# Inverse roots as exp(-0.5 ln x) on ScalarE, the squares one step sooner, and no filler products on TensorE

## The reference

```
def _l2norm(t):
    n = jnp.sqrt(jnp.sum(t * t, axis=-1, keepdims=True))
    return t / jnp.maximum(n, EPS)
q = _l2norm(proj(Wq, bq));  k = _l2norm(proj(Wk, bk));  v = proj(Wv, bv)     # 16 heads of 8
attn = einsum('bhid,bhjd->bhij', q, k) / n ** sigmoid(m)                      # no softmax
x = x + (attn @ v) @ Wo + bo
x = x + cross_attention(ctx, ctx, layernorm(x))      # feature maps exp(z), exp(-z), then a softmax
x = x + ffn(layernorm(x))                            # shared expert and 16 routed experts, top 1
def _layernorm(x):  return (x - mean) / jnp.sqrt(var + 1e-5)
```

## Time and profile before

| | |
|---|---|
| median of 3 runs | 513.48 us (512.52 to 515.56) |
| profiled execution, its own time | 517.45 us |
| its span, first to last instruction | 515.6 us |
| phase 1, from the first statistics to the last copy into `xT` | 3.99 to 117.13 us |
| one full step of phase 1 | 12.13 us |
| mean granted clock of PE over the span | 0.921 of full speed |

### The profile page before, as it was taken

How to read it: one execution, slowest core, us unless ns; L and a number is a source line. 1 busy time by engine, 2 the same in 40 slices (tenths; PEclk the granted TensorE clock), 3 DMA queues, 4 the chain that set the end, 5 groups by cost and what they waited for, 6 DMA issues and landing times.

```text
span 515.6 us, 10998 instructions
## 1 busy us (share of the span) xinstructions
PE 429.5 (83%) x3804; PEld 322.7 (63%) x3804; DVE 298.8 (58%) x886; ACT 263.1 (51%) x603; POOL 201.7 (39%) x280
## 2 busy tenths in 40 slices
PE   2788888777777389999998999799999998888890
PEld 1466566554444268888888887595566666767650
DVE  4777877632665667787877773725733332444434
ACT  5465555347777417777776777424722222333320
POOL 1322222214886626455552000000377501777730
PEclk9999999987888759999998999857999997999996
DMA  6830000001899967667771000000051103788629
GB/s 207 298 97 1 0 0 1 1 0 53 240 259 278 330 160 189 170 180 181 187 198 44 7 4 5 2 0 0 17 175 52 47 1 83 223 286 273 217 63 294
DMA packets 50353, 62.21 MB, mean 121 GB/s; under 512 B 7316, under 2 KB 46772, under 8 KB 48692
## 3 DMA queue, kind: packets, MB, share of 16 engines
q1 hardware_dynamic: 38528, 37.89, 25.1%
q0 software_dynamic: 4864, 20.43, 14.3%
q10 hardware_dynamic: 6912, 3.25, 2.6%
HBM read 43.68 MB, written 20.73 MB: 125 GB/s over the span
## 4 chain that ended last, share of the span: by engine, by line
PE 54%; DVE 15%; ACT 9%; issue 8%; DMA 7%; SPq 5%; ACTq 1%; POOL 0%; DVEq 0%; POOLq 0%
PE bank L709 6%; PE bank L698 5%; PE bank L1234 5%; PE bank L1235 5%; PE bank L1224 4%; PE bank L671 3%; PE bank L1279 3%; DVE mx L778 2%; PE bank L1218 2%; PE bank L733 2%; PE bank L410 2%; PE bank L434 2%; DMA qparts<-qpart 2%; PE bank L397 2%; ACT t_hT L1159 1%
## 5 line engine op out<-in xcount | busy, mean ns | idle before, releaser
L867 ACT ACTIVATE prob<-bank 77x512 f32<-77x512 f32 x128 | 74.3, 595 | 23.4 <-PE bank L698 23.3
L778 DVE TENSOR_REDUCE mx<-bank 128x5 f32<-128x385 f32 (+1 forms) x96 | 54.9, 576 | 18.7 <-PE bank L671 16.0
L1202 POOL DMA_INDIRECT sorted_in<-h_rows,pos_s x32 | 31.5, 986 | 85.9 <-DVE pos_s L1054 76.5
L1207 POOL DMA_INDIRECT routed<-t_y,t_no x48 | 46.4, 966 | 40.8 <-DVE t_y L1092 31.1
L698 PE MATMUL bank<-qst,kst 99*77 99x128 bf16 x512 | 51.0, 223 | 0.2 <-ACT prob L867 0.2
L698 PEld LDWEIGHTS bank<-qst,kst 99*77 99x77 bf16 x512 | 39.2, 117 | 7.8 <-ACT prob L867 3.9
L377 POOL TENSOR_TENSOR qkv<-qkv,rn 128x256 f32<-128x256 f32 x32 | 19.1, 629 | 63.4 <-DVE rn L296 63.4
L1008 DVE TENSOR_TENSOR act<-bank,s_g 128x512 f32<-128x512 f32 x28 | 19.3, 691 | 42.1 <-ACT s_g L1147 42.0
L671 PE MATMUL bank<-kst,qst 96*128 96x77 bf16 x512 | 36.2, 208 | 7.3 <-DVE mx L778 3.7
L1147 ACT ACTIVATE s_g<-bank 128x512 f32<-128x512 f32 x28 | 16.7, 597 | 48.6 <-PE bank L1235 48.6
L1224 PEld LDWEIGHTS bank<-sd,act 128*128 128x128 f32 x224 | 29.2, 192 | 14.9 <-issue 12.3
(11 more groups left out here) (167 smaller groups left out, 1033.3 us busy)
## 6 DMA issues: line engine op xcount, KB each, us to landing
qst<-qparts POOLq DMA_DIRECT2D x36, 256.0 KB, 3.5
t_w<-in_expert_w SPq DMA_DIRECT2D x48, 192.0 KB
qparts<-qpart SPq DMA_DIRECT2D x16, 384.0 KB, 7.7
kst<-kparts POOLq DMA_DIRECT2D x36, 154.0 KB, 3.9
kparts<-kpart SPq DMA_DIRECT2D x16, 231.0 KB, 7.9
sorted_in<-in_fill SPq DMA_DIRECT2D x1, 3168.0 KB, 13.4
t_row<-sorted_in ACTq DMA_DIRECT2D x48, 66.0 KB
qst<-qparts SPq DMA_DIRECT2D x12, 256.0 KB, 6.5
```

The costliest lines, as they stand in the source:

```text
L778: v.tensor_reduce(mx[:, b % JA, h0:h1], bank[n % 2][:, 0:(h1 - h0) * KEYS].rearrange("p (h k) -> p h k", k=KEYS), AX.X, ALU.max, negate=Tr ...
L867: a.activation(prob[n % PROBS][:].rearrange("p c t -> p (c t)"), bank[2 + n % 2][0:KEYS], ACT.Exp, scale=SCORE_SCALE).then_inc(s["expd"], 1)
L1202: p.indirect_dma_start(out=sorted_in, out_offset=bass.IndirectOffsetOnAxis(ap=pos[:, b:b + 1].bitcast(U32), axis=0), in_=h_rows[:, b], in_ ...
L1207: p.indirect_dma_start(out=routed, out_offset=bass.IndirectOffsetOnAxis(ap=t_no[r][:].bitcast(U32), axis=0), in_=t_y[r][:], in_offset=None ...
```

## The change

Four edits:

1. Every inverse root of a norm is now exp(-0.5 ln x). For the three layer norms ACT runs Ln of the variance plus eps and then Exp with scale -0.5, both on the four (or 28) values, and DVE has only the bias left. For q and k DVE clamps the sum of squares (with the square of the old limit), then ACT runs Ln and Exp on 128x128 and writes `rn` itself. The reciprocals on DVE go.
2. ACT's table is asked for once, at the start, as one that holds both Ln and Exp. The program now has two table loads: that one (L199 of the changed kernel) and Silu (L1150).
3. The squares of a group are taken one step sooner, at the end of its `front` step behind the copy of `qT`, no more at the head of its `middle` step. On DVE the second layer norm's bias moves in between the second and third addition of the qkv bias.
4. `keep_streaming` is gone.

```diff
 dve_phase1
-            def scale_and_bias(g, k, std_s, rstd_s, bias_s):
-                v.wait_ge(s[std_s], g + 1)
-                v.reciprocal(ln_rstd[k][:], ln_std[k][:]).then_inc(s[rstd_s], 1)
+            def bias(g, k, rstd_s, bias_s):
                 v.wait_ge(s[rstd_s], g + 1)
                 v.scalar_tensor_tensor(out=ln_bias[k][:], in0=ln_mv[k][:, :, 0], scalar=-1.0, in1=ln_rstd[k][:],
...
+                    v.wait_ge(s["ss1"], g + 1)
+                    v.tensor_scalar(ss[:], ss[:], L2_EPS * L2_EPS, None, ALU.max).then_inc(s["nmax1"], 1)
                 if first:
-                    scale_and_bias(first[0], 0, "std1", "rstd1", "bias1")
-                if middle:
-                    v.wait_ge(s["nrm1"], g + 1)
-                    v.tensor_scalar(nrm[:], nrm[:], L2_EPS, None, ALU.max).then_inc(s["nmax1"], 1)
-                    v.wait_ge(s["nmax1"], g + 1)
-                    v.reciprocal(rn[:], nrm[:]).then_inc(s["rn1"], 1)
+                    bias(first[0], 0, "rstd1", "bias1")
...
                     statistics(g, 1, "stat2", "mean2")
-                    scale_and_bias(g, 1, "std2", "rstd2", "bias2")
                 if front:
...
+                    for j in range(JP // 2):
+                        add_qkv_bias(front[0], front[1], j)
+                if back:
+                    bias(back[0], 1, "rstd2", "bias2")
+                if front:
+                    for j in range(JP // 2, JP):
+                        add_qkv_bias(front[0], front[1], j)
 act_phase0 and act_phase1
+            a.preload_act_table_set("natural_log_exp_and_others")
...
             def step(first, front, middle, back):
-                if middle:
-                    g, par, _ = middle
-                    a.wait_ge(s["qkv1"], g * JP + JP)
-                    a.activation(sq[:], qkv[par][:, :, 0:2 * D], ACT.Square).then_inc(s["sq1"], 1)
                 if front:
...
                 if first:
-                    deviation(first[0], 0, "mean1", "std1")
+                    log_variance(first[0], 0, "mean1", "log1")
                 if middle:
-                    a.wait_ge(s["ss1"], middle[0] + 1)
-                    a.activation(nrm[:], ss[:], ACT.Sqrt).then_inc(s["nrm1"], 1)
+                    a.wait_ge(s["nmax1"], middle[0] + 1)
+                    a.activation(nrm[:], ss[:], ACT.Ln).then_inc(s["nrm1"], 1)
+                if first:
+                    inverse_deviation(first[0], 0, "log1", "rstd1")
+                if middle:
+                    a.wait_ge(s["nrm1"], middle[0] + 1)
+                    a.activation(rn[:], nrm[:], ACT.Exp, scale=-0.5).then_inc(s["rn1"], 1)
...
                 if back:
                     g, par, _ = back
-                    deviation(g, 1, "mean2", "std2")
+                    log_variance(g, 1, "mean2", "log2")
+                    inverse_deviation(g, 1, "log2", "rstd2")
                     normalise(g, 1, "bias2", xn2[par], "xn2")
...
+                if front:
+                    g, par, _ = front
+                    a.wait_ge(s["qkv1"], g * JP + JP)
+                    if not is_first(g):
+                        a.wait_ge(s["ss1"], g)
+                    a.activation(sq[:], qkv[par][:, :, 0:2 * D], ACT.Square).then_inc(s["sq1"], 1)
 pe_phase1
-                    keep_streaming(2)
...
-                    keep_streaming(3)
 phase 3
-            inverse_root(v, 0)
+            v.wait_ge(s["rstd3"], 1)
...
-            inverse_root(v, 1)
+            v.wait_ge(s["rstd3"], 2)
...
-            a.activation(std[:, lo:hi], mv[:, lo:hi, 1], ACT.Sqrt, bias=eps[:]).then_inc(s["std3"], 1)
+            a.activation(std[:, lo:hi], mv[:, lo:hi, 1], ACT.Ln, bias=eps[:]).then_inc(s["log3"], 1)
+            a.wait_ge(s["log3"], k + 1)
+            a.activation(rstd[:, lo:hi], std[:, lo:hi], ACT.Exp, scale=-0.5).then_inc(s["rstd3"], 1)
```

More of the change, by code:

```diff
@@ L139, in decoder_layer @@
                   "ones_rows", "ones_in", "set", "tavp", "rden", "avn", "t2p", "t2", "fcp", "x2", "stat3", "mean3",
-                  "xb2", "std3", "xn3", "h_kept", "hTp", "hT", "lgp", "rstd3", "lg", "r_step", "oh", "rankp",
+                  "xb2", "log3", "xn3", "h_kept", "hTp", "hT", "lgp", "rstd3", "lg", "r_step", "oh", "rankp",
                   "escore", "sc_ready", "pos", "rows", "scat", "etile", "gup", "silu", "act", "downp", "x3", "tTp",
@@ L279, in scale_and_bias, with add_qkv_bias @@
                                        op0=ALU.mult, op1=ALU.mult).then_inc(s[bias_s], 1)
+            def add_qkv_bias(g, par, j):
+                v.wait_ge(s["qkvp"], g * JP + (j + 1))
+                v.tensor_tensor(qkv[par][:, j], bank[1 + j][:, 0:3 * D], bqkv[:], ALU.add).then_inc(s["qkv1"], 1)
             def step(first, front, middle, back):
@@ L321, in act_phase1, with log_variance, inverse_deviation @@
         def act_phase1(a):
-            def deviation(g, k, mean, std_s):
+            def log_variance(g, k, mean, log_s):
                 a.wait_ge(s[mean], g + 1)
-                a.activation(ln_std[k][:], ln_mv[k][:, :, 1], ACT.Sqrt, bias=eps[:]).then_inc(s[std_s], 1)
+                a.activation(ln_std[k][:], ln_mv[k][:, :, 1], ACT.Ln, bias=eps[:]).then_inc(s[log_s], 1)
+            def inverse_deviation(g, k, log_s, rstd_s):
+                a.wait_ge(s[log_s], g + 1)
+                a.activation(ln_rstd[k][:], ln_std[k][:], ACT.Exp, scale=-0.5).then_inc(s[rstd_s], 1)
             def normalise(g, k, bias_s, dst, done):
@@ L386, in pe_phase1 @@
         def pe_phase1(pe):
-            def keep_streaming(n):
-                for _ in range(n):
-                    pe.matmul(bank[0][:, 0:3 * D], ident[:], wqkv[:], start=True, stop=True)
             def step(first, front, middle, back):
@@ L962, in deviation3 @@
             a.wait_ge(s["mean3"], hi)
-            a.activation(std[:, lo:hi], mv[:, lo:hi, 1], ACT.Sqrt, bias=eps[:]).then_inc(s["std3"], 1)
-        def inverse_root(v, k):
-            lo, hi = NORMED[k]
-            v.wait_ge(s["std3"], k + 1)
-            v.reciprocal(rstd[:, lo:hi], std[:, lo:hi]).then_inc(s["rstd3"], 1)
-            v.wait_ge(s["rstd3"], k + 1)
+            a.activation(std[:, lo:hi], mv[:, lo:hi, 1], ACT.Ln, bias=eps[:]).then_inc(s["log3"], 1)
+            a.wait_ge(s["log3"], k + 1)
+            a.activation(rstd[:, lo:hi], std[:, lo:hi], ACT.Exp, scale=-0.5).then_inc(s["rstd3"], 1)
         def normalise3(v, g):
```

## The result

| | before | after |
|---|---|---|
| median of the timed runs | 513.73 us (512.52 to 515.56) | 506.62 us (505.41 to 509.09) |
| profiled execution, its span | 515.6 us | 503.6 us |
| mean granted clock of PE over the span | 0.921 | 0.909 |
| last copy into `xT` begins (end of phase 1) | 116.5 us | 107.9 us |

A second set of six runs of the same kernel gave 0.9882 (0.9829 to 0.9935); its median is 7.2 us less by the five fast runs that the ratio goes by, and 4.7 with the sixth, of 515.0 us, which counts as slow because it lies over 1.5% above the fastest.

The account below looks back on a forecast made before the run. Phase 1 was taken as bound by latency through DVE and ACT. Start and tables -1.3, full steps -6.2, draining steps -2.7 and -3.4, clock +10.4 sum to -3.2, giving a median of 510.3 us, range 501.5 to 517.

Parts of the forecast that it names:

- ring: Phase 1's repeating chain of handovers through PE, ACT and DVE, 12.14 us a full step, forecast to shorten by 1.24.
- draining steps: Two steps near the end of phase 1, forecast to fall from 11.74 to 9.0 and 11.75 to 8.3 us.
- clock term: Phase 1 without filler: PE's clock falls to half in nearly every step, 1.3 us each over eight steps, +10.4.
- Full step at full clock, 10.90: One full phase 1 step takes 10.90 us against 12.14 while PE's clock holds; five steps give -6.2.
- The clamp and the 0.95 us reciprocal gone from ahead of L302 give -0.98: In a full step, DVE's attention addition starts 2.86 us behind the output product instead of 3.84.
- Start and tables, -1.3: Four of six ACT table loads go; the exposed one at the start gives 1.28 us, the others nearly nothing.
- Sum at full clock, -13.6: Start, full steps and draining steps of phase 1 together, before any loss through PE's clock: -13.6 us.
- the fall at 103.0: Earlier trace's drop of PE to half clock after a 1.99 us wait, taken as sign for falls in nearly every step.
- a clock that stays down: Rival: phase 1 runs at half clock throughout, +10 to +20, 524 to 533 us; chance 0.17 with its milder form.
- one that holds throughout: Rival: PE's clock stays up in phase 1 and most or all of -13.6 remains, 500 to 506 us; chance 0.17.
- falls rarely: Form of the held-clock rival: few falls in phase 1, 500 to 506 us; within its chance of 0.17.
- my own case: Likeliest case: the clock falls in most phase 1 steps and 1 to 7 us are gained; chance 0.40.

Follow-up runs that it names:

- e2: The change with three filler PE products back ahead of the transposes of `xn2`: 14.2 us less than the kernel before (0.9750).
- e10: The change with one filler PE product ahead of the transposes of `xn2`: 13.6 us less than the kernel before (0.9758).
- e4: e2 with POOL's addition of the output bias cut to 8 of 128 features, leaving work out: 15.3 us less than the kernel before (0.9710).
- e7: e2 with POOL's addition of the output bias put behind the second layer norm's bias: 497.96 us, 16.3 less than the kernel before (0.9679).
- e11: e7 with an unread 128x128 reciprocal on DVE ahead of the attention addition: 13.4 us less than the kernel before (0.9783).
- e9: e7 with one filler product instead of three in the draining steps: 15.2 us less than the kernel before (0.9722).
- e5: The kernel before with only the squares taken one step sooner, fillers kept: 4.4 us less (0.9899).
- e6: e2 with the squares back at the head of the `middle` step: 9.6 us less than the kernel before (0.9784).
- e8: The change without the request for the common Ln and Exp table: 594.62 us in a single run, 30 more than the kernel before.
- e1: The change with both fillers back, two products ahead of k and v and three ahead of `xn2`'s transposes: 7.6 us less than the kernel before (0.9857).
- e3: The kernel before with both fillers removed and nothing else changed: 7.1 us more (1.0131).

## Why the prediction was right, and what was mis-sized

**Direction and mechanism: right.** A ring shortened by the DVE work that leaves it, draining steps that gain most, and part of it given back through the clock. The median of 506.6 lies 3.7 us below the 510.3 forecast, and that is the size of the clock term, not of the ring.

**Full step at full clock, 10.90: right.** 10.95 in the change and in e2, e10. L301 is 2.99 us behind the product (2.86 forecast), the second bias ends with POOL's addition, ACT's queue sets the end. The reading that POOL holds the second bias was tested by e4 and e7: 0.42 us a step.

**"The clamp and the 0.95 us reciprocal gone from ahead of L302 give -0.98": -0.85 measured** (3.84 to 2.99). e11 adds that such an operation isn't worth its duration in this place, as it fills a gap and overlaps its neighbours.

**Draining steps, 9.0 and 8.3: right.** 9.18 and 8.12 at full clock (e9, e10). e5 and e6 show that the second is the squares' place, 3.2 to 3.3 us, where I had counted the reciprocal too; part of this, an estimated 0.6 to 1.2 us, is the half clock of that step.

**Start and tables, -1.3: consistent.** The logarithm starts at 5.59 where the root started at 6.72, and the first `xn` 1.1 us sooner. How much of this reaches the first output product the runs don't settle: it starts 0.8 us sooner in one profiled execution of the change and 1.5 in the other. The loads at L537, L963 and L1140 show next to nothing: the lead is 8.7 us at the last `xT`, 8.8 at the transposes of phase 3 and 8.9 at the first gate product of phase 4 (349.7 before, 340.8 now). e8 shows how much hangs on the one line that asks for the common table.

**Sum at full clock, -13.6: right.** With full steps of 10.95 (the fifth 10.85), draining steps of 9.18 and 8.12 and the first product where e2 has it (24.39; the profiled kernels with edits 1 to 3 have it between 23.87 and 25.75), the last one stands at 96.3, and the last `xT` 6.5 us later at 102.8: 13.7 us ahead of before. By the medians e2 with its filler has -14.2, 12.4 of it in phase 1.

**The clock term, +10.4 ("a fall in nearly every step", 1.3 us each): mis-sized, and the step that failed.** Against e2 the missing filler costs 7.0 us by the first set's median (-7.1) and 6.9 by the second's (-7.2), or 9.5 with its longest run. In phase 1, against the last `xT` at full clock (102.8), it is 5.0 us in the first profiled execution (107.9) and 10.4 in the second (113.3). Both factors were wrong, and their errors partly cancel. A fall is dearer than 1.3 us: it stays for 10.2 us and costs 2.3 to 2.6 in full steps and 4.9 where it reaches over the draining steps. And it is rarer: one in the five full steps in one execution, three in another, never in neighbouring steps. So the 10.4 that the second execution shows is three dear falls and not eight cheap ones, and that it equals the forecast is luck. I had taken the stay from the shortest stretch of the earlier trace rows and the frequency from one resemblance, the fall at 103.0. From 25 to 58 us of the first trace PE had the waits that I described, and the clock stayed.

What makes it fall in one step and not in the next, the traces don't show. Of the rivals, a clock that stays down is refuted for this kernel, and so is one that holds throughout. The other form of that rival, a clock that "falls rarely" with 500 to 506 us, is what the first profiled execution shows: one fall in the full steps and 505.4 us. The median, 506.6, lies between that rival and my own case. e2, which holds the clock by other means, shows what holding it is worth: 513.7 - 14.2 = 499.5.

**Not settled.** Kernels gain or lose 0.1 to 3 us between the last `xT` and the end of phase 3 (e1 5.2 us ahead at the one, 8.1 at the other) and again in phase 4. PE's low-clock stretches lie elsewhere in each, but no run isolates this. It is why e1 and e5 gained 2 us more than phase 1 shows.

## What to carry to other kernels

A chain of hand-overs through three engines is shortened only by what stands on it, and less than by its duration where there are gaps or overlap beside it; the draining steps may gain more than the steady ones. PE products that nobody reads cost nothing while PE is the one who waits, and keep its clock; they should be taken out only after their number and their place have been tried, since here one or three at one place were worth some 7 us and two at another cost 0.9 us a step. A tiny operation on DVE with a long duration in the trace is worth comparing with what POOL does at that time: one wait for the right order gave another 2 us.

## What the runs showed of the hardware

- The change's ten runs spread from 505.4 to 515.0 us, those of e7, whose clock stays up until 103 us in its trace, from 497.4 to 498.6. The three longest are those with the lowest mean clock of the span (0.888 to 0.895: 512.1 to 515.0 us; the other seven, 0.900 to 0.914: 505.4 to 509.1).
- Once fallen in a full step of the change, the clock stayed low for 10.2 us, in all four falls of the two traces, though PE was busy 8.86 of 10.30 us (first trace, at 67.2). In e3 the falls lasted 6.8 to 13.7 us. In the earlier trace rows it rose after 3.4 us in which PE was busy throughout.
- e4, e6 and e10 each had a fall at about 25 us, in the first step, and e2, e7, e9 and e11 none there, although e2 and e4 differ by nothing but the size of one addition on POOL. Each of these kernels has one trace.
- In two of the three sets the gate products of phase 4 took 106 to 109 us from the first to the last instead of 74, in every profiled kernel, with a median of 0.59 us for one of them in all sets. What differed is open.
